# Layer 3's rows gathered in units 9 to 12, and unit 1's B split and gathered earlier, in a four-layer conditioned residual stack

## The reference, cut to what matters

```python
x = x + (einsum('bct,bcd->bdt', x, w0[idx_a]) + bias0[idx_a][:, :, None])   # layer 0
def lora_linear(x, W, A, B):                                               # layer 1
    return x @ W + (x @ A[idx_a]) @ B[idx_a]
gate, up = lora_linear(x, Wg, Ag, Bg), lora_linear(x, Wu, Au, Bu)           # 512 -> 2048
x = x + lora_linear(silu(gate) * up, Wd, Ad, Bd)                            # 2048 -> 512
x = x + (x @ W2.T + ((x @ A2[idx_b].T) @ B2[idx_b].T) * scal[idx_b])        # layer 2
x = x + einsum('bct,bcd->bdt', x, w3[idx_c])                                # layer 3
```

## Time and profile before

| | us |
|---|---|
| median of 3 runs without the profiler | 722.78 (720.82 to 723.44) |
| profiled execution, its own time | 726.11 |
| its span, first to last instruction | 724.3 |

### The profile page before, as it was taken

The page is one execution under the profiler, slowest core; times in us unless marked ns, Lnnn a source line. Parts: engine busy times, 40 slices in busy tenths (PEclk is TensorE's granted clock), DMA queues, the critical chain, the costliest instruction groups (busy, mean ns, idle before and its releaser), DMA issues.

```text
span 724.3 us, 10882 instructions
## 1 busy us (share of the span) xinstructions
PE 695.9 (96%) x3647; PEld 592.1 (82%) x3647; DVE 557.8 (77%) x977; ACT 263.8 (36%) x476; POOL 335.8 (46%) x606
## 2 busy tenths in 40 slices
PE   7989799999999999999879999999999999999997
PEld 6767688888888888888667888888888888799997
DVE  9778678787887888699866878786978785975553
ACT  3644224242323242334223242422433231345554
POOL 5966525353434344439173545454453434235541
PEclk9999899999999999999998999999999999999999
DMA  8479523333334242504752232323332316023432
GB/s 214 127 201 234 195 89 108 119 110 116 120 105 133 86 131 81 109 9 160 243 126 81 79 103 84 103 84 104 110 107 76 101 50 205 23 83 108 132 117 95
DMA packets 91895, 84.39 MB, mean 117 GB/s; under 512 B 44736, under 2 KB 73664, under 8 KB 91840
## 3 DMA queue, kind: packets, MB, share of 16 engines
q1 hardware_dynamic: 80128, 52.73, 24.4%
q0 software_dynamic: 11392, 30.95, 14.1%
q10 hardware_dynamic: 320, 0.02, 0.0%
HBM read 70.57 MB, written 13.11 MB: 116 GB/s over the span
## 4 chain that ended last, share of the span: by engine, by line
PE 82%; DVE 7%; issue 4%; ACT 2%; POOL 2%; another core or an unknown queue 1%; POOLq 1%; ACTq 0%; DVEq 0%
PE bank L1749 38%; PE bank L1876 22%; PE bank L1757 6%; PE bank L1886 4%; PE bank L2010 3%; PE bank L2016 3%; PE bank L1989 2%; PE bank L2049 1%; POOL w0second L532 1%; POOLq L565 1%; DVE XC L1211 1%; PE bank L1727 1%; POOL tmp L582 1%; DVE XA L1357 1%
## 5 line engine op out<-in xcount | busy, mean ns | idle before, releaser
L1749 PE MATMUL bank<-XC,WC 128*128 128x512 f32 x1344 | 335.7, 396 | 10.1 <-ACT tmp L829 3.9
L1749 PEld LDWEIGHTS bank<-XC,WC 128*128 128x128 f32 x1344 | 245.6, 190 | 59.1 <-ACT tmp L829 4.3
L1876 PE MATMUL bank<-hs,wds 128*128 128x512 f32 x768 | 186.2, 391 | 0.1
L1876 PEld LDWEIGHTS bank<-hs,wds 128*128 128x128 f32 x768 | 142.0, 188 | 28.8 <-DVE wds L1299 0.5
L560 POOL DMA_INDIRECT BL<-bgtab,poffs x96 | 99.1, 1032 | 131.1 <-PE bank L1757 90.9
L560 POOL DMA_INDIRECT BL<-butab,poffs x96 | 96.7, 1008 | 82.7 <-PE bank L1757 61.8
L1357 DVE TENSOR_TENSOR XA<-bank,XA 128x512 f32<-128x512 f32 x128 | 87.0, 686 | 21.1 <-PE bank L1876 15.2
L845 ACT ACTIVATE hs<-hid 128x512 fp32r<-128x512 f32 x64 | 40.1, 629 | 172.5 <-DVE hid L1340 100.0
L839 ACT ACTIVATE hid<-hid 128x512 f32<-128x512 f32 x48 | 30.3, 633 | 152.3 <-DVE hid L1323 79.3
L604 POOL COPY adsel<-ad_raw 128x32 f32 x256 | 44.3, 224 | 71.6 <-DVE ads L1304 67.8
L1757 PEld LDWEIGHTS bank<-UT,BL 128*128 128x128 f32 x384 | 61.9, 192 | 13.2 <-issue 5.1
(11 more groups left out here) (215 smaller groups left out, 852.0 us busy)
## 6 DMA issues: line engine op xcount, KB each, us to landing
RW<-in_L_cond_Wg_dram SPq DMA_DIRECT2D x16, 512.0 KB
RW<-in_L_cond_Wu_dram SPq DMA_DIRECT2D x16, 512.0 KB
RD<-in_L_cond_Wd_dram SPq DMA_DIRECT2D x16, 512.0 KB
out_dram<-XB SPq DMA_DIRECT2D x15, 256.0 KB, 2.0
XB<-in_x_dram SPq DMA_DIRECT2D x8, 256.0 KB, 5.6
x1park<-XB SPq DMA_DIRECT2D x8, 256.0 KB
x2park<-XA SPq DMA_DIRECT2D x8, 256.0 KB
XA<-x1park SPq DMA_DIRECT2D x4, 512.0 KB, 6.5
```

The source lines that it names most:

```text
L1749: last = nc.tensor.matmul(psum[:, :], WC[:, t, left, a, k, :], XC[:, right, b, k, :], start=(first and k == 0 and n == 0), stop=(k == 1 an ...
L1876: last = nc.tensor.matmul(psD[j % 2][:, :], by_feature(wds[:, f, a, :])[:, j % KT, :], hs[:, f, b, j // KT * 512:(j // KT + 1) * 512], sta ...
```

## The change

Layer 3's row gathers leave units 8 and 13: they stand in units 9 to 12, four in each. B of unit 1 is split right behind layer 0's last instructions on ScalarE and VectorE, ahead of unit 0's gate window, and its store is issued on SP right behind its load, ahead of Ad's eight loads. On GpSimd `gather_b(2, 0)` changes places with `select_ad(0)`.

```diff
                 load_d(0)
                 load_b(1)
+                store_b(1)
 
                 sp.wait_ge(s_xr[0], SUMMED)
@@
-                    if unit + 1 < UNITS:
+                    if unit and unit + 1 < UNITS:
                         store_b(unit + 1)
@@
                     gather_b(b + 1, 1)
-                    if unit == 0:
-                        select_ad(unit, cols)
                     if unit + 1 == ALL:
                         continue
                     gather_b(b + 2, 0)
+                    if unit == 0:
+                        select_ad(unit, cols)
@@
-                    if h and i < 6:
-                        if i == 0:
+                    if h and 1 <= i <= 4:
+                        if i == 1:
                             pool.wait_ge(s_offs, 1)
                             pool.wait_ge(s_xcl, 14)
-                        for p in range(3 * i, min(3 * i + 3, PAIRS)):
+                        for p in range(4 * (i - 1), 4 * i):
@@ scalar
-                    if unit + 1 < UNITS:
+                    if unit and unit + 1 < UNITS:
                         b_high(unit + 1)
@@
                 xr_copy(HP + 6)
                 xr_copy(HP + 7)
+                b_high(1)
                 for unit in range(ALL):
@@ vector
-                    if unit + 1 < UNITS:
+                    if unit and unit + 1 < UNITS:
                         b_low(unit + 1)
@@
                 u_own(0, 2)
                 u_own(0, 3)
+                b_low(1)
                 for unit in range(ALL):
```

## The result

| | before | after |
|---|---|---|
| median without the profiler, 22 runs each | 721.39 (716.89 to 728.96) | 718.41 (716.10 to 722.17) |
| profiled execution, its own time | 726.11 | 717.85 |
| its span | 724.3 | 716.0 |

The ratio is 0.9959 (95% interval 0.9943 to 0.9976): 3.0 us faster, not the 13.8 forecast. The two profiled executions stand further apart, 8.3 us of span, because the one of before was a slow draw: 4.7 us over the median of its kernel.

A forecast was written before the change was run, and what follows sets the result against it. TensorE, busy 695.9 of 724.3 us, was taken as the bound, leaving only its waits and half clock to win. Unit 9's 8.0 and unit 1's 5.8 off the 722.78 median gave 709.0 us; 8-in-10 range 706.0 to 724.5, forecast's chance 0.36.

The forecast's parts named there:

- Unit 9, the mechanism: Unit 9's stall goes with GpSimd's unbroken string of fifteen gathers, ending as the last lands; splitting it into two of six removes it.
- Unit 9, the size: Removing unit 9's stall was to save 8.0 us of its 42.89; 0 if the stall doesn't go with the string.
- unit 9 returns to 34.92: Unit 9, first of the second half, was to take an undisturbed unit's 34.92 us in place of 42.89.
- Unit 1, Ad and the gathers: Unit 1: Ad lands and its columns start at 68.5 (66.5 to 70.5); gather_b(2, 1) issued by 76.1, 1.7 later.
- slower case through SP's queue: Ad's loads wait behind the store that waits for VectorE; Ad at 74.5, unit 9 as before: 726.5 us, chance 0.18.
- Unit 1, the landing: Unit 1's last gathered rows land at 78.4, product ready at 77.1: TensorE idles 1.3 us in place of 3.7.
- To their landing I add 2.3 us: Unit 1: time from the end of gather_b(2, 1)'s issue at 76.1 to landing at 78.4; quiet case 1.6.
- first rival: Only unit 9's stall goes, as the parkings still fill the DMA engines in unit 1: 714.8 us, chance 0.13.
- Unit 1, the floor: Unit 1 was to cost an undisturbed unit's 34.92 plus 1.3 idling plus 0.4 small gaps, no half clock counted.
- Unit 1, what it would have been worth: Unit 1 was to shrink by 5.8 us from 42.46; bounds 7.5 less to 0 less.
- B's split early at no cost: Unit 0: B lands at 49.5, lora matmuls come 0.2 late, covered by 1.43 us of waiting; a landing at 53 costs 2.
- ceiling: Units 1 and 9 stand 7.5 and 8.0 us over the undisturbed unit; 15.5 us is the most the change can win.

The follow-up runs named there:

- before_again: The kernel before, unchanged, profiled a second time on the first chip: median 723.67 us, ratio 1.0014; unit 1 40.18, unit 9 41.96 us.
- b_only: Kernel before with only B of unit 1 split, stored and gathered early, layer 3's rows left in place; first chip: 723.08 us, ratio 1.0009.
- b2_late_3: Kernel before with b2's four small-packet loads issued in unit 9 instead of unit 8; fourth chip, one run: 726.58 us, unit 9 42.85.
- b_only_2: Kernel before with only B's early split, store and gather, run on the fourth chip: 723.09 us, ratio 1.0002; unit 9 37.64 us.
- after_again: The changed kernel once more, on the first chip: 717.03 us, ratio 0.9920 to the kernel before; unit 1 40.14, unit 9 35.86 us.
- w3_only: Kernel before with only layer 3's rows moved to units 9 to 12; first chip: 716.97 us, ratio 0.9927; unit 1 37.80, unit 9 35.89.
- w3_park_late_2: Kernel before with layer 3's rows in units 9 to 12 and x1's parkings issued in unit 1 instead of unit 0; fourth chip: 714.18 us, ratio 0.9895.
- after_third: The changed kernel on the fourth chip: 716.78 us, ratio 0.9928 to the kernel before; unit 1 40.84, unit 9 35.92 us.
- before_third: The kernel before, unchanged, profiled on the third chip, one run: 714.9 us; unit 9 35.9 us, no stall there.
- after_park_late: The changed kernel with x1's eight parkings issued in unit 1 instead of unit 0; second chip: 713.78 us, ratio 0.9998 to before; unit 1 37.28.
- w3_one_3: Kernel before with one layer 3 row gather in unit 8 and three in each of units 9 to 13; fifth chip, one run: 718.89 us.
- pool_busy_2: Kernel before with layer 3's rows in units 9 to 12 and sixteen small GpSimd copies in their old place in unit 8; fifth chip: 719.58 us.

## Why the prediction was right and wrong

*Unit 9, the mechanism: right as far as it reaches.* The prediction took the stall for the work of the unbroken string and put its end at the landing of the last gather, as an inference from two places. Four profiles with the string and a stall of full length (the first one, before_again, b_only, b2_late_3) give 1.76 to 1.77 us from the end of the string to the end of the wait, b_only_2 cuts the string and the wait with it, and none of twelve profiles with a broken string had the wait in unit 9, six of them on the three chips where such stalls were seen (two of the six on the fifth, where unit 9's stall is inferred). That the two units share one mechanism is likely and not shown. With nine gathers cut to six the wait for "remote" in unit 1 is gone (silu on time at 76.53, 75.52, 75.63, 75.48 in four profiles with B's part, 1.2 us late in after_again), but it was missing with nine in w3_only and w3_park_late_2 too. The prediction also passed over the string of nine in unit 0 of the same trace, whose silu was on time. What it left out is that the string needs the chip as well, and in unit 1 something that differs from one execution to the next. How a string on GpSimd holds up the products' semaphores stays open; that GpSimd and VectorE too saw their product late in b_only_2 says that it isn't a matter of ScalarE.

*Unit 9, the size: 8.0 forecast, 7.0 measured, 6.1 on another chip.* The step that failed is the floor, "unit 9 returns to 34.92". 34.92 is unit 2; unit 9 takes 35.9 without a stall, in every kernel. TensorE is busy for 35.67 of it, so this unit has more work inside these cuts, 0.75 us, and unit 10 has not. The other 0.9 between the chips goes with the clock: half for 6.8 us from 379.5 in the first profile (0.92 in the earlier trace rows), for 3.4 in before_again (0.96).

*Unit 1, Ad and the gathers: right.* Forecast and measured: Ad's columns start 68.5 and 68.76 (bounds 66.5 to 70.5), gather_b(2, 1) issued by 76.1 and 76.29, no slower case through SP's queue. The price for loads moved 5.3 us later was worked out well.

*Unit 1, the landing: wrong. This is the step that failed and cost the most: 40.35 us where 37.28 are reached without the parkings.* "To their landing I add 2.3 us", for a product at 78.4 and 1.3 us of idling; it was 3.90, 80.19, 2.63 and half clock. In four profiles with the parkings beside the gathers the time from the end of the issue to the first use is 3.90, 4.19, 4.35 and 3.92 (after, b_only, after_third, b_only_2), and 4.40 in after_again, where the late silu had a part; in the one without them it is 1.86. The 2.3 was read in the kernel before as the time to the moment when its DMA engines fell still, at 80.6, for a gather issued 5 us behind the last parking (254 GB/s on the mean until then). But the prediction itself had moved the parkings 4.3 us later, to about 70 to 79, on top of the gathers, and had named the full engines (357 GB/s in 70 to 77) as a ground for its first rival. It moved the transfers and kept a landing time read where they weren't. The Trainium skill, "DMA: Bandwidth & Descriptors", "Issuing engines are not separate DMA queues", says that transfers of all issuers interleave on the same 16 engines; the runs agree (on the second chip 1.86 us at 87 GB/s and 4.02 at 258), and the prediction applied it to Ad's loads and not to the last gathers. The 2.0 us of fixed cost in the same page's "Anatomy of one DMA — SWDGE (gpsimd) path", from which it drew a sentence that agreed with its 78.4, is borne out here only while the engines are quiet (1.78 and 1.86 us).

*Unit 1, the floor: wrong too.* The sum took 34.92 + 1.3 + 0.4, so 36.6. TensorE is busy for 36.2 of unit 1 at full clock (36.20 in before_third and in after_park_late), 1.3 more than in unit 2. The 3.7 between 36.6 and 40.35 are this floor with 1.3, half clock, which the prediction counted as none, with 1.3 (TensorE busy for 37.50 and not 36.20), and idling with 1.15 (2.85 in all in place of 1.7).

*Unit 1, what it would have been worth: over-sized too.* 42.46 was one execution. Other profiles of kernels with B as before give 37.8 to 42.9 there, and 40.18 for before_again on the first chip. With B's part and the parkings beside it, it is 40.1 to 41.1. A wait for a late semaphore was changed for a wait for data of the same size; in executions without late semaphores just the new wait would be left, which is not shown: no kernel with B's part and the early parkings ran on the second or third chip.

*B's split early at no cost: nearly.* B landed at 50.2 and not 49.5; ScalarE's silu came at 52.27, and the lora matmuls at 53.37 in place of 51.35. The cover named for it (1.43 us of TensorE's idling before 53.37) took most; 0.7 us was left in the profile of after. Not all of it is B's: 1.42 us of the silu's delay are the wait for "remote", and in b_only, after_third and b_only_2, whose silu came at 50.55 to 50.62, unit 1 starts at 68.80 to 68.86, no later than in the profile of before.

*The sum.* The prediction's ceiling was 15.5. Reachable, by the best values seen, were 42.89 - 35.89 and 42.46 - 37.28, so 12.2. The profiled execution reached 8.3, the kernel after, by its ratios, 3.0, 5.8 and 5.2 (first pair, first chip, fourth chip). That is the first rival, "only unit 9's stall goes", by its mechanism and by its sign; its time of 714.8 was 3.6 too low. Of this, 1.0 is the floor of unit 9 and 1.4 the median of before, 721.39 over 22 runs against 722.78 over 3. The rest stays open: one can think of executions of before in which unit 9 stalls briefly, as in b_only_2, but profiles of single executions can't count them.

## What to carry to other kernels

When a step moves transfers later, read the landing time of everything that lands in their new place again: the latency behind an issue here was 1.8 to 1.9 us on quiet DMA engines and 2.8 to 4.4 us beside bulk stores, and with the clock that fell behind it the difference was 3 of the 5.8 us forecast. The floor of a stretch is the same stretch without the disturbance, not its neighbour, and a stall seen in one execution on one chip is worth its mean over executions and chips. If engines see finished products late while GpSimd issues gathers back to back, try breaking the string with something that waits, and profile the kernel before more than once: the same instructions stalled in one execution and not in the next.

## What the runs showed of the hardware

Finished TensorE products were seen up to 6.8 us late by ScalarE, and kept GpSimd waiting for 1.7 us, around strings of nine to fifteen indirect gathers with 0.30 us between them. The wait ended 1.5 to 1.8 us behind the last of the string in unit 9 and in four profiles of unit 1, and 0.1 behind it in before_again. It did so on three chips of five (on the fifth in units 0 and 1; its two profiles have no longer string), there not in every execution, and on the two others the same instructions with the same spacing delayed nothing. The same program took 714 to 715 us there and 721 to 727 on the others. The cause of the difference isn't known. Behind every idle stretch of TensorE of 2.6 us or more in units 1 and 9 its granted clock fell to 0.50, for 3.4 us (after, b_only, after_third, b_only_2, w3_one_3, pool_busy_2, unit 9 of before_again) or 6.8 us (the first profile, b2_late_3), after idling of the same length: 3.91 us at unit 9's drop in b_only and in b2_late_3. In the two with 6.8 us it fell while TensorE was still idle (at 379.5 in the first profile, 1.6 us ahead of its next product). Shorter idling went either way: 1.62 us in unit 0 of w3_park_late_2, and 1.22 and 0.93 us close together in unit 1 of after_again, were followed by half clock, 2.08 us in unit 1 of before_again and 1.98 in unit 9 of b_only_2 were not.
